# Attention's normalised x turned without TensorE: ScalarE regroups, VectorE turns 32x32 blocks, four DMAs place them

## The reference

```python
q = (layernorm(x) @ Wq.T + bq)   # split into 16 heads of 32
k = (ctx @ Wk.T + bk);  v = (ctx @ Wv.T + bv)
scores = einsum('bhqd,bhkd->bhqk', q, k) * 32 ** -0.5   # masked, causal
out = softmax(scores) @ v                                # heads joined
x = x + tanh(g_xattn) * (out @ Wo.T + bo)
xn = layernorm(x);  xp = xn shifted by one token
r = sigmoid((mu_r * xn + (1 - mu_r) * xp) @ W_r.T)
k = (mu_k * xn + (1 - mu_k) * xp) @ W_k.T
x = x + tanh(g_ffn) * (r * (relu(k) ** 2 @ W_v.T))
```

## Time and profile before

| | |
|---|---|
| median of 3 runs | 1876.82 us (1875.66 to 1877.02) |
| the profiled execution: its time | 1877.37 us |
| its span, first to last instruction | 1875.6 us |
| granted TensorE clock, mean | 0.996 of full speed |
| PE busy | 1843.8 us, 98% |
| DVE busy | 1372.9 us, 73% |
| POOL busy | 1142.2 us, 61% |
| ACT busy | 1069.8 us, 57% |
| DMA queue q1 | 241.07 MB, 49.7% of 16 engines |

### The profile page before, as it was taken

One profiled execution on the slowest core, in us unless ns is written; L12 is line 12 of the kernel. 1 busy time (PEld: TensorE's weight loads), 2 busy tenths in 40 slices (PEclk: granted clock), 3 DMA queues, 4 the chain that ended last, 5 costly groups with the idle time before them and its releaser, 6 DMA issues.

```text
span 1875.6 us, 35183 instructions
## 1 busy us (share of the span) xinstructions
PE 1843.8 (98%) x10928; PEld 1449.0 (77%) x10928; DVE 1372.9 (73%) x3732; ACT 1069.8 (57%) x2055; POOL 1142.2 (61%) x1833
## 2 busy tenths in 40 slices
PE   6999999999999999999999999999999999999999
PEld 5677777777777777777777777777678888888887
DVE  6776777677676777677677677767688787888864
ACT  5655555565555556555565555556575555656562
POOL 2777777777677777767777777776652423233231
PEclk9999999999999999999999999999999999999999
DMA  7555465445546545554645556465244535353421
GB/s 220 105 133 129 125 159 122 129 122 143 132 113 163 124 119 127 143 148 100 163 114 124 134 130 156 114 159 141 68 135 124 146 108 162 100 149 112 140 86 68
DMA packets 159801, 243.32 MB, mean 130 GB/s; under 512 B 22752, under 2 KB 51424, under 8 KB 158848
## 3 DMA queue, kind: packets, MB, share of 16 engines
q1 hardware_dynamic: 159616, 241.07, 49.7%
HBM read 92.06 MB, written 33.59 MB: 67 GB/s over the span
## 4 chain that ended last, share of the span: by engine, by line
PE 94%; DVE 3%; issue 1%; DMA 1%; POOL 0%; ACT 0%; SPq 0%; DVEq 0%; ACTq 0%
PE proj_ps L41 15%; PE proj_ps L42 15%; PE proj_ps L43 15%; PE score_ps L1446 10%; PE prob_ps L1470 8%; PE value_ps L1489 8%; PE score_ps L41 3%; PE score_ps L43 3%; PE score_ps L42 3%; PE sum_ps L1497 2%; PE sum_ps L43 1%; PE sum_ps L41 1%; PE sum_ps L42 1%; PE value_ps L41 1%; PE value_ps L43 1%; PE value_ps L42 1%
## 5 line engine op out<-in xcount | busy, mean ns | idle before, releaser
L1089 DVE CUSTOM_DVE_ANT_0 score_ps<-score_ps,causal 128x128 f32<-128x128 f32 (+3 forms) x1024 | 488.8, 505 | 291.5 <-PE score_ps L1446 291.4
L692 ACT ACTIVATE probs<-prob_ps 128x512 f32<-128x512 f32 (+1 forms) x768 | 396.1, 528 | 368.6 <-PE prob_ps L1470 184.6
L1446 PE MATMUL score_ps<-k_stack,q_stack 97*128 97x128 f32 (+3 forms) x1024 | 318.9, 353 | 4.5 <-DVE least L1089 3.6
L1470 PE MATMUL prob_ps<-q_stack,k_stack 100*128 100x512 f32 (+3 forms) x1024 | 280.5, 314 | 2.8 <-DMA q_stack<-max_rows 2.7
L563 POOL TENSOR_TENSOR kact<-square,kact 128x512 fp32r<-128x512 f32 x64 | 96.0, 1510 | 306.3 <-ACT kact L778 306.3
L495 POOL TENSOR_TENSOR prob_sum<-probs 128x384 f32<-128x384 f32 x256 | 260.0, 1016 | 0.0
L1446 PEld LDWEIGHTS score_ps<-k_stack,q_stack 97*128 97x128 f32 x1024 | 187.5, 189 | 75.1 <-issue 39.8
L498 POOL TENSOR_TENSOR prob_sum<-prob_sum,probs 128x256 f32<-128x256 f32 x256 | 198.2, 774 | 37.0 <-POOL prob_sum L495 0.4
L1470 PEld LDWEIGHTS prob_ps<-q_stack,k_stack 100*128 100x128 f32 x1024 | 192.0, 191 | 22.3 <-DMA q_stack<-max_rows 3.3
L484 POOL TENSOR_SCALAR_AFFINE_SELECT probs<-probs 128x256 f32<-128x256 f32 x256 | 104.7, 409 | 152.7 <-ACT probs L692 152.7
L488 POOL TENSOR_SCALAR_AFFINE_SELECT probs<-probs 128x256 f32<-128x256 f32 x256 | 106.8, 417 | 125.1 <-ACT probs L692 125.1
(11 more groups left out here) (180 smaller groups left out, 4665.2 us busy)
## 6 DMA issues: line engine op xcount, KB each, us to landing
k_stack<-staged SPq DMA_DIRECT2D x384, 128.0 KB
q_stack<-staged SPq DMA_DIRECT2D x384, 128.0 KB, 3.1
x_io<-in_x SPq DMA_DIRECT2D x16, 1024.0 KB, 7.9
x<-x_io SPq DMA_DIRECT2D x64, 256.0 KB, 3.1
res<-x SPq DMA_DIRECT2D x64, 256.0 KB, 3.4
out_x<-res SPq DMA_DIRECT2D x64, 256.0 KB, 5.4
tiles<-in_x SPq DMA_DIRECT2D x15, 1024.0 KB, 5.4
tiles<-in_ctxT SPq DMA_DIRECT2D x60, 256.0 KB, 3.9
```

Source lines behind the costliest of these rows:

```text
L692: nc.scalar.activation(probs[:, u % RING, lo:hi], prob_ps[(3 * u + c) % 2][:, 0:hi - lo], ACT.Exp, scale=SCALE).then_inc(exp_done, 1)
L1089: nc.vector.tensor_tensor_reduce(out=here, in0=here, in1=causal[:, LATE - P * t:S], scale=-1.0, scalar=3e38, op0=ALU.add, op1=ALU.min, acc ...
L1446: last = nc.tensor.matmul(here[:, at:at + P * (t + 1)], q_stack[n][0:MASK_ROW + 1, j, P * t:P * t + P], k_stack[n][0:MASK_ROW + 1, j, 0:P ...
L1470: last = nc.tensor.matmul(here[:, at:at + width], k_stack[n][0:ROWS, j, P * k:P * k + P], q_stack[n][0:ROWS, j, P * k:S], start=True, stop ...
```

## The change

For batches 1 to 15 of attention the normalised x is no longer turned on PE. `load_x` brings 32 tokens of each quarter of 128 to 32 partitions, in four DMAs. ACT's `apply_layernorm` writes its result 128 columns to the left and regroups it, so that words that were 4 apart stand side by side in groups of 32 (it writes with a step of 32 words). DVE turns all 32x32 blocks in four new instructions (`turn_normalised`) in `second` of slot 8, each waiting for the one before. Four DMAs of 256 KB (`move_normalised`) bring each quarter of tokens to 128 partitions of x_room[1], which is the room of xT's low part, so they wait for q3; SP issues two before and two behind the `stack_q` of slot 9. ACT and DVE make the high and low part from there instead of from PSUM. xT is now kept by quarters, and the query projections read it as four blocks of 128 columns. The banks' order and the waits follow: PE's transposes of x1 to x15 and the wait for xt_low in `values` are gone, `load_c` waits for the four moves.

For room x_io has three rows instead of four: residual tiles 0, 1 and 3 are loaded one by one in slot 1, tile 2 in slot 8 into the row of tile 0, and POOL adds the bias to tile 2 in slot 10. In the FFN the blocks that DVE turns lie in the room of wo's low part, no longer in x_io. WORK is unchanged; its entries x0+ to x3+ do nothing before batch 16.

```diff
         ident = sb("ident", [P, P])
-        tiles = sb("tiles", [P, T, D])
-        x_io = sb("x_io", [P, T, D])
+        turning = sb("turning", [P, T, P + D])
+        tiles = turning[:, :, P:P + D]
+        x_io = sb("x_io", [P, 3, D])
...
+        ln_turned, ln_moved = sem("ln_turned"), [sem(f"ln_moved{a}") for a in range(QUARTERS)]
...
+        res_loaded = [sem(f"res_loaded{m}") for m in range(T)]
...
-                if 0 <= b < B:
+                if 0 <= b < B and (name[0] != "x" or b == 0):
...
-        x_blocks = x_io[:].rearrange("p t d -> p (t d)").rearrange("p (n m c) -> p n m c", m=T, c=SIDE)
+        x_blocks = wo_room[1][:].rearrange("p t d -> p (t d)").rearrange("p (n m c) -> p n m c", m=T, c=SIDE)
+
+        def x_row(b, m):
+            return turning[:, :, 0:P] if (b, m) == (B - 1, 2) else x_io[:, (0, 1, 0, 2)[m], :]
+
+        def as_row(here, b, m):
+            return here.rearrange("p (n c) -> p n c", n=T) if (b, m) == (B - 1, 2) else here
+
+        def quarter(tensor, a):
+            return tensor[:].rearrange("p k n -> p (k n)")[:, K * P * a:K * P * a + K * P]
+
+        def by_quarters(tensor, k):
+            return tensor[:].rearrange("p k n -> p (k n)").rearrange("p (a k n) -> p a k n", a=QUARTERS, k=K)[:, :, k, :]
+
+        def turned_on_tensor(b):
+            return T * (0 if b == 0 else b - B + 1)
...
+                elif b < B:
+                    for a in range(QUARTERS):
+                        here = x[b, P * a:P * a + P].rearrange("(m c) d -> c m d", c=SIDE)
+                        sp.dma_start(tiles[SIDE * a:SIDE * a + SIDE], here).then_inc(x_loaded, 16)
                 else:
-                    here = (x[b] if b < B else x1[b - B]).rearrange("(t p) d -> p t d", p=P)
-                    sp.dma_start(tiles[:] if b <= B else x_in[:], here).then_inc(x_loaded, 16)
+                    here = x1[b - B].rearrange("(t p) d -> p t d", p=P)
+                    sp.dma_start(tiles if b <= B else x_in[:], here).then_inc(x_loaded, 16)
+
+            def move_normalised(b, a):
+                sp.wait_ge(ln_turned, K * b)
+                sp.wait_ge(q_done, K * b)
+                sp.dma_start(quarter(x_room[1], a), tiles[SIDE * a:SIDE * a + SIDE]).then_inc(ln_moved[a], 16)
...
             def load_c(b, k):
-                sp.wait_ge(xt_done, T * b + k + 1)
+                for a in range(QUARTERS):
+                    sp.wait_ge(ln_moved[a], 16 * b)
                 sp.dma_start(tiles[:, k, :], ctxT[b, P * k:P * k + P]).then_inc(c_loaded[k], 16)
...
-            def load_residual(b):
-                for m in range(T if b > 0 else 0):
-                    sp.wait_ge(x1_stored[m], 16 * b)
-                sp.dma_start(x_io[:], x[b].rearrange("(t p) d -> p t d", p=P)).then_inc(res_loaded, 16)
+            def load_residual(b, m):
+                if m == 2 and b < B - 1:
+                    sp.wait_ge(x1_stored[0], 16 * (b + 1))
...
+                elif b > 0:
+                    sp.wait_ge(x1_stored[2 if m == 0 else m], 16 * b)
+                elif m < 2:
+                    sp.wait_ge(mask_stored, 16)
+                sp.dma_start(x_row(b, m), as_row(x[b, P * m:P * m + P], b, m)).then_inc(res_loaded[m], 16)
...
+                sp.dma_start(as_row(x1[b, P * m:P * m + P], b, m), x_row(b, m)).then_inc(x1_stored[m], 16)
...
                 if has_prev and s == 1:
-                    load_residual(b - 1)
+                    for m in (0, 1, 3):
+                        load_residual(b - 1, m)
+                    if b == B:
+                        load_residual(b - 1, 2)
+                if has_prev and s == 8:
+                    load_residual(b - 1, 2)
+                if has_next and s == 9:
+                    move_normalised(b + 1, 0)
+                    move_normalised(b + 1, 1)
...
+                if has_next and s == 9:
+                    move_normalised(b + 1, 2)
+                    move_normalised(b + 1, 3)
...
             def add_residual_bias(b, m):
-                pool.wait_ge(res_loaded, 16 * (b + 1))
-                nc.gpsimd.tensor_tensor(x_io[:, m, :], x_io[:, m, :], bo_gated[:], ALU.add).then_inc(res_ready, 1)
+                pool.wait_ge(res_loaded[m], 16 * (b + 1))
+                nc.gpsimd.tensor_tensor(x_row(b, m), x_row(b, m), as_row(bo_gated[:], b, m), ALU.add).then_inc(res_ready, 1)
...
-                if s in (2, 3) and 0 <= b - 1 < B - 1:
-                    add_residual_bias(b - 1, 2 * (s - 2))
-                    add_residual_bias(b - 1, 2 * (s - 2) + 1)
+                if s == 2 and 0 <= b - 1 < B - 1:
+                    add_residual_bias(b - 1, 0)
+                    add_residual_bias(b - 1, 1)
+                if s == 3 and 0 <= b - 1 < B - 1:
+                    add_residual_bias(b - 1, 3)
+                if s == 10 and 0 <= b - 1 < B - 1:
+                    add_residual_bias(b - 1, 2)
...
             def apply_layernorm(b, m):
                 act.wait_ge(ln_step, NORM_STEPS * (b + 1))
-                here = x_tile(b, m)
-                nc.scalar.activation(here, here, ACT.Identity, bias=newton[:, 3, m:m + 1], scale=newton[:, 1, m:m + 1]
+                here = there = x_tile(b, m)
+                if 0 < b < B:
+                    here = here.rearrange("p (k c g) -> p k c g", k=K, g=QUARTERS)
+                    there = turning[:, m, 0:D].rearrange("p (k g c) -> p k c g", k=K, g=QUARTERS)
+                nc.scalar.activation(there, here, ACT.Identity, bias=newton[:, 3, m:m + 1], scale=newton[:, 1, m:m + 1]
                                      ).then_inc(ln_applied, 1)
...
             def high_part_x(b, m):
-                act.wait_ge(xt_done, T * b + m + 1)
-                if b > 0:
+                if b == 0:
+                    act.wait_ge(xt_done, m + 1)
+                    nc.scalar.copy(quarter(xT[0], m), bank(f"x{m}")[:]).then_inc(xt_high, 1)
+                else:
+                    act.wait_ge(ln_moved[m], 16 * b)
                     act.wait_ge(q_done, K * b)
-                nc.scalar.copy(xT[0][:, :, P * m:P * m + P], bank(f"x{m}")[:].rearrange("p (k n) -> p k n", k=K)
-                               ).then_inc(xt_high, 1)
+                    nc.scalar.copy(quarter(xT[0], m), quarter(x_room[1], m)).then_inc(xt_high, 1)
...
+                elif b < B:
+                    dve.wait_ge(x_loaded, 16 * QUARTERS * b)
                 elif b < B + BY_DMA:
-                    dve.wait_ge(x_loaded, 16 * b)
+                    dve.wait_ge(x_loaded, 16 * QUARTERS * (B - 1) + 16 * (b - B + 1))
...
-                    for n in range(T):
-                        dve.wait_ge(x1_stored[n], 16 * B)
+                    dve.wait_ge(o_done, T * B)
...
             def low_part_x(b, m):
                 dve.wait_ge(xt_high, T * b + m + 1)
-                nc.vector.tensor_tensor(xT[1][:, :, P * m:P * m + P], bank(f"x{m}")[:].rearrange("p (k n) -> p k n", k=K),
-                                        xT[0][:, :, P * m:P * m + P].bitcast(F32), ALU.subtract).then_inc(xt_low, 1)
+                here = bank(f"x{m}")[:] if b == 0 else quarter(x_room[1], m)
+                nc.vector.tensor_tensor(quarter(xT[1], m), here, quarter(xT[0], m).bitcast(F32), ALU.subtract).then_inc(xt_low, 1)
+
+            def turn_normalised(b, k):
+                dve.wait_ge(ln_applied, T * (b + 1))
+                wait(dve, ln_turned, K * b - 1 - k)
+                nc.vector.transpose(out=tiles[:, :, P * k:P * k + P].rearrange("p g (m c) -> p m g c", c=SIDE),
+                                    in_=turning[:, :, P * k:P * k + P].rearrange("p m (g c) -> p m g c", c=SIDE)
+                                    ).then_inc(ln_turned, 1)
...
                 dve.wait_ge(o_done, T * b + m + 1)
-                dve.wait_ge(res_ready, T * b + m + 1)
-                nc.vector.scalar_tensor_tensor(out=x_io[:, m, :], in0=o_bank(b, m)[:], scalar=gate[:, 0:1],
-                                               in1=x_io[:, m, :], op0=ALU.mult, op1=ALU.add).then_inc(o_added, 1)
+                dve.wait_ge(res_ready, T * b + (1, 2, 4, 3)[m])
+                nc.vector.scalar_tensor_tensor(out=x_row(b, m), in0=as_row(o_bank(b, m)[:], b, m), scalar=gate[:, 0:1],
+                                               in1=x_row(b, m), op0=ALU.mult, op1=ALU.add).then_inc(o_added, 1)
...
+                if has_next and b >= 0 and s == 8:
+                    for k in reversed(range(K)):
+                        turn_normalised(b + 1, k)
+                if has_next and b >= 0 and s == 11:
                     low_part_x(b + 1, 2)
...
-                if g == 1 and b + 1 < B:
-                    pe.wait_ge(xt_low, T * (b + 2))
-                elif g == 1:
+                if g == 1 and b + 1 == B:
                     pe.wait_ge(xt_copied, T)
...
-                                     lambda k: [part[:, k, :] for part in xT], [k], k == 0, k == K - 1)
+                                     lambda k: [by_quarters(part, k) for part in xT], [k], k == 0, k == K - 1)
```

(2 more changed lines are left out.)

30 lines of the change are left out of this document (15 added, 15 removed).

## The result

The changed kernel takes 1896.06 us in the median (1893.25 to 1901.22, 4 runs), beside it the kernel before 1876.74 us (1875.66 to 1877.02, 4 runs): a ratio of 1.0107, 95% interval 1.0084 to 1.0130. It is 19 us slower. The forecast was 5 us faster, and the range ended at 1886. The profiled execution, the fastest of the four, took 1893.25 us with a span of 1891.5, 15.9 more than before, at a granted TensorE clock of 0.993 (before 0.996).

What follows compares the result with a forecast made beforehand. TensorE (PE), busy for 98% of the span, was taken as the bound. 15 batches x 0.35 = 5.3 us off the profiled 1877.4 gives 1872.1; the median is 0.5 lower, so 1871.6 us, range 1865 to 1886.

Steps and rivals of the forecast that it cites:

- The queue of SP ... Price here: nothing.: SP's queue, slots 9 to 11: maxima issued at about 643.0 behind the moves; PE may be 0.9 us late at no cost.
- rival 3: Slot 11: maxima arrive late behind 512 KB of moves, up to 4.86 us from issue; slower, 1889 us; chance 0.13.
- Slot 10 gives 0.46 to 0.50 us: PE in slot 10: 0.80 us of transposes go, but turn_maxima then waits for VectorE's split, leaving 0.46 to 0.50 us gained.
- never less than 1.89 us: Slot 11: VectorE's add_output(2) and max1 keep last o2 start to scores (11, 2) at 1.89 us or more, against 2.00 today.
- VectorE's work: VectorE: low parts collide with POOL and delay o2's addition, 0.16 us lost per batch; four slot 8 transposes, 2.9 us, cost nothing.
- ScalarE's write: apply_layernorm's strided write on ScalarE: taken as 0.81 us as now; up to twice that nearly free.
- the fourth rival: ScalarE's strided write takes three times its length, 2.4 us, delaying exponents and the maxima copy; about 1909 us; chance 0.05.
- The q matmuls: Query matmuls on PE reading four blocks of 128 columns: taken as 0, upper bound perhaps 10 ns x 720 = 7 us.
- PE's busy time: Sign in the new profile: PE busy down by some 23 us, but the span by 5.

Runs made afterwards that it cites:

- half_moves: Changed kernel with four moves of 128 KB instead of 256 KB, the casts reading another tile (output incomplete): 1877.72 us, ratio 0.9999 to the kernel before.
- without moves: Changed kernel with its four moves per batch left out, the low and high parts reading another tile (output wrong): 1876.83 us, ratio 0.9999 to the kernel before.
- plain_write: Changed kernel with ScalarE writing the normalised x in plain order, the regrouping of columns left out: 1896.76 us, ratio 1.0099 to the kernel before.

## Why the prediction was wrong, and where it was right

**The step that failed: "The queue of SP ... Price here: nothing."** It named the right wait, order and place. From the start of the q stack's issue it put the maxima's issue 3.1 us on (639.88 to 643.0). It was 4.02 (402.26 to 406.28). The missing 0.9 us are the q stack's three issues, 2.51 instead of the 1.84 of the earlier trace rows, and two gaps of 0.1. In half_moves the same distance is 3.40 (396.93 to 400.33): 0.3 of the 0.9 come with the issues, 0.6 only with the full bytes. The arrival, 3.59 us from issue, was inside the 3.75 taken as free. The point from which PE is late was nearly right: 3.1 + 3.75 puts it 6.9 us after the q stack's issue. PE asked 6.51 us after it (408.77), and with the 0.61 that the gate of max1 makes it wait anyway nothing would be lost up to 7.1; the prediction had 0.9 for this slack. The maxima came after 7.61, and this batch's 8 to 12 is 20.70, 0.44 longer than before and 0.55 longer than without moves. So the mis-sized term is SP's time to issue, read from a stretch without moves (DMA share 0.48 from 639 to 647) and used for one behind 512 KB of them (0.91). The counter-argument to the rival, that its 4.86 us arrival had three times the bytes ahead, looked at the arrival alone. And the step priced one typical batch and one wait: besides it there are the longer waits in slot 11 of some batches, 12 to 0 (3.0 us), and batch 0 (4.3 us), where half comes with the lower clock. That rival 3, at 1889, came nearer is in part luck: it had the late arrival as its cause, and no clock and no slot 13 in it.

**Slot 10: a second step that failed, "Slot 10 gives 0.46 to 0.50 us".** The turn of the maxima begins 0.22 us after the split (403.94 to 404.16) as read from the earlier trace rows. Without moves the last scores of slot 10 stand 1.40 us after the first, before 1.86 (641.05 to 642.91, in the stretch of the earlier trace rows): the 0.46 forecast. But the next matmul, o2's first, waits for the low part of k3 in its bank, which 0.28 us behind the scores had never shown. It stands 0.60 behind them, and the matmul after it 0.1 later still; 0.03 of the 0.46 is left. This alone would have taken most of the forecast gain, with no moves at all.

**Slot 11: right.** From the last o2 to scores (11, 2) "never less than 1.89 us": without moves it is 1.88 (402.96 to 404.84), with an idle of 0.60 or 0.61 put down to `least`, in every batch from the second on. This gives 0.1 us a batch, and in the time nothing that can be measured, where 5.3 us were forecast. In the changed kernel the gate is hidden behind the later `max_rows`.

**VectorE's work: near in size, wrong in effect.** The groups of the low parts and the transposes:

```profile
L1123 DVE TENSOR_TENSOR xT_low<-xT_room_low,xT_high 128x512 fp32r<-128x512 f32 x60 | 52.7, 879 | 5.6 <-ACT xT_high L701 5.6
L1128 DVE STREAM_TRANSPOSE turning<-turning 128x512 f32<-128x512 f32 x60 | 42.7, 712 | 5.6 <-ACT turning L684 0.5 <-DVE turning L1128 0.5
```

The first two low parts take 0.95 and 1.17 us beside POOL's sums and its addition, which itself takes 1.74 us instead of 1.29; the last two take 0.70 and 0.69. But the addition of o2, which they were said to delay by 0.16, waits for PE (0.18 us), since o2 is late by the gate above. The four transposes take 3.17 us in slot 8 where 2.9 were reckoned (0.79 apart, not 0.75), and the idle before the correction is 0.54 us as it was 0.53: free, as said.

**ScalarE's write: longer than the 0.81 us taken, free as said.** 1.32 us instead of 0.81, inside the bound of twice, and free, as plain_write shows. The rule of the Trainium skill (SBUF — State Buffer, Door 1: The DMA port swizzle), that accesses to new 16-byte lines pay, agrees with this row in its sign; it isn't the three times of the fourth rival.

**The q matmuls** with their four blocks of columns start 0.22 to 0.24 us apart, as before: 0, as taken. The 10 ns of the upper bound had no row behind it.

**PE's busy time** fell by 10 us, not by 23. It is made of modelled ends, and matmuls behind a stall show 0.50 instead of 0.39; the count (240 fewer) and the distances of starts are what can be read.

## What to carry to other kernels

Before bytes are taken from an engine that computes and given to the DMA engines, read the DMA share of the very stretch, not of the span, and beside it how long the waiting engine leaves the small DMA behind it: here 0.48 and 4.2 us, with room for half a megabyte and none for the second half, while the share of the queue over the span went only from 49.7% to 55.1%. A small DMA on which an engine waits is priced by its issue and its arrival together, both at the load after the change. Moving it in the order brought back 15 of 19 us here and left a wait further on; moving it to ScalarE's queue lost 41 us in a kernel without any moves. And removing work from the bounding engine pays only after each bank and buffer behind it has been followed to who frees it: a gap of 0.3 us that was never a wait becomes one.

## What the hardware showed beyond that

- SP's time to issue three DMAs of 128 KB grew from 1.84 (no moves) and 1.90 (half moves) to 2.51 and 2.73 us behind the full ones. The engines' share alone doesn't explain it: before the change three such issues took 1.83 us at 648.05, in a stretch (647 to 654) with a share of 1.02. What makes an issue slow was not settled.
- The same 8 KB DMA, issued at the same moment after its copy, reached PE 6.2 us after issue through ScalarE's queue in a batch of the kernel before, and within 4.69 through SP's; the kernel lost 2.2% by that edit alone.
- ScalarE's write of 512 float32 with a step of 128 bytes took 1295 ns in the mean against 804 ns in plain order (64 each, with the four of batch 0, which are plain in both).
- In batch 0 of the changed kernel the granted TensorE clock was at 0.5 from 78.8 to 89.0 us; it fell during a wait of PE of 3.58 us; 12 to 0 took 23.5 us there instead of 21.3, with no wait of PE in it.
- VectorE's transposes of 128x512 took 712 ns each from and to the same tile; four in a row, each waiting for the one before, took 3.17 us, 0.79 apart.
